# Centred values from TensorE, weight halves ahead of the gates, and a first tile list from four groups

## The reference

```python
q = layernorm(x); k = v = ctx
ig = concat(q, k, v) @ igate_kernel + igate_bias        # one value per token and head
fg = concat(q, k, v) @ fgate_kernel + fgate_bias
log_D = cumsum(log_sigmoid(fg)) - transpose(cumsum(...)) + transpose(ig)   # lower triangle
D = exp(log_D - max(log_D));  C = (q @ k.T / 8) * D
h = (C / (max(|sum C|, exp(-max)) + 1e-6)) @ v
h_norm = (h - mean(h)) * rsqrt(var(h) + 1e-5) * outnorm_scale   # over the 64 features of a head
x = x + h_norm
y = layernorm(x);  top 2 of softmax(y @ router_w.T), weights scaled to sum 1
x = x + sum over the 2 experts of  weight * (gelu(y @ w1[e]) @ w2[e])      # 256 to 1024 to 256
```

## Time and profile before

| what | value |
|---|---|
| time, median of 3 runs | 681.55 us (680.57 to 682.21) |
| profiled execution, its own time | 682.88 us |
| its span, first to last instruction | 681.1 us |
| mean granted TensorE clock | 0.92 of full |
| PE busy | 573.2 us (84%) |
| DVE busy | 400.2 us (59%) |
| ACT busy | 303.1 us (45%) |
| POOL busy | 253.9 us (37%) |
| DMA moved | 118.20 MB |

### The profile page before, as it was taken

How to read it: one execution, slowest core, us unless ns; L and a number is a source line. 1 busy time by engine, 2 the same in 40 slices (tenths; PEclk the granted TensorE clock), 3 DMA queues, 4 the chain that set the end, 5 groups by cost and what they waited for, 6 DMA issues and landing times.

```text
span 681.1 us, 17983 instructions
## 1 busy us (share of the span) xinstructions
PE 573.2 (84%) x5872; PEld 462.7 (68%) x5880; DVE 400.2 (59%) x1146; ACT 303.1 (45%) x585; POOL 253.9 (37%) x194
## 2 busy tenths in 40 slices
PE   1786787777888189979999699989999999999992
PEld 1464566565766178868877578867888888887881
DVE  1469788787887536566567345545555555554550
ACT  2465734626353034544454344434444444444441
POOL 1132238567584405544525422212232233322321
PEclk9796988878787579989999989989999999999997
DMA  9888996694252913636474826598432933295322
GB/s 305 295 322 287 388 323 217 242 322 188 89 209 76 374 56 74 193 71 186 83 194 82 253 43 175 122 328 261 84 53 49 290 50 52 50 319 141 52 25 23
DMA packets 55531, 118.20 MB, mean 174 GB/s; under 512 B 6000, under 2 KB 38000, under 8 KB 54448
## 3 DMA queue, kind: packets, MB, share of 16 engines
q1 hardware_dynamic: 39344, 96.75, 41.0%
q0 software_dynamic: 13392, 18.10, 15.0%
q10 hardware_dynamic: 2736, 2.64, 1.1%
HBM read 188.49 MB, written 40.13 MB: 336 GB/s over the span
## 4 chain that ended last, share of the span: by engine, by line
PE 62%; DVE 11%; issue 7%; ACT 6%; DMA 6%; POOL 3%; SPq 2%; ACTq 1%; DVEq 0%; POOLq 0%
PE bank L706 16%; PE bank L686 9%; PE bank L688 9%; PE bank L687 9%; PE bank L708 8%; PE bank L535 4%; DMA wring<-wsplit 3%; PE bank L609 3%; PE bank L667 2%; ACT xn L795 2%; DVE oh L1132 1%; DVE ct L1029 1%; POOL rows L1462 1%; POOL hrs L1454 1%; DMA rw_all<-in_router_t 1%
## 5 line engine op out<-in xcount | busy, mean ns | idle before, releaser
L1491 POOL DMA_INDIRECT out<-yo,dst x71 | 113.8, 1603 | 286.1 <-DMA out<-yo,dst 156.4
L686 PE MATMUL bank<-wcv,wring 128*128 128x128 f16 x1136 | 202.2, 222 | 16.0 <-DVE wcv L1267 10.1
L1283 DVE TENSOR_TENSOR wcv<-wcv 128x512 f16<-128x512 f32 x142 | 98.3, 692 | 181.8 <-ACT wcv L890 118.8
L687 PE MATMUL bank<-wcv,wring 128*128 128x128 f16 x1136 | 202.3, 222 | 0.0
L688 PE MATMUL bank<-wcv,wring 128*128 128x128 f16 x1136 | 202.3, 222 | 0.0
L706 PE MATMUL bank<-wring,wcv 128*128 128x512 f16 x568 | 193.6, 381 | 0.0
L888 ACT ACTIVATE wcv<-bank 128x512 f32<-128x512 f32 x142 | 84.8, 597 | 213.6 <-PE bank L688 204.2
L708 PE MATMUL bank<-wring,wcv 128*128 128x256 f16 x568 | 155.3, 273 | 0.0
L686 PEld LDWEIGHTS bank<-wcv,wring 128*128 128x128 f16 x1136 | 112.7, 99 | 33.4 <-issue 18.7
L687 PEld LDWEIGHTS bank<-wcv,wring 128*128 128x128 f16 x1136 | 112.7, 99 | 1.5
L688 PEld LDWEIGHTS bank<-wcv,wring 128*128 128x128 f16 x1136 | 112.8, 99 | 0.0
(11 more groups left out here) (148 smaller groups left out, 752.8 us busy)
## 6 DMA issues: line engine op xcount, KB each, us to landing
wring<-wsplit SPq DMA_DIRECT2D x284, 512.0 KB
wring<-in_w SPq DMA_DIRECT2D x16, 1024.0 KB, 12.6
xrow<-rows SPq DMA_DIRECT2D x71, 130.0 KB
wsplit<-wring SPq DMA_DIRECT2D x4, 2048.0 KB, 7.7
wsplit<-wcv SPq DMA_DIRECT2D x4, 2048.0 KB, 7.6
xa<-in_x SPq DMA_DIRECT2D x8, 512.0 KB, 9.4
kT<-in_ctx_t SPq DMA_DIRECT2D x8, 512.0 KB, 8.7
ctn<-in_ctx SPq DMA_DIRECT2D x8, 512.0 KB, 8.6
```

The source lines that it names most:

```text
L686: pe.matmul(o, hi, xT[k][:, c, :], start=(c == 0), stop=False)
L687: pe.matmul(o, hi, xT[k][:, CK + c, :], start=False, stop=False)
L1283: dve.tensor_tensor(gl[o % 2][a][:, :, :], gf[a].rearrange("p (m n) -> p m n", m=4), gh[o % 2][a][:, :, :], ALU.subtract).then_inc(s_glo, 1)
L1491: pool.indirect_dma_start(out=out[:, :], out_offset=bass.IndirectOffsetOnAxis(ap=dst[o][:, 0:1], axis=0), in_=yo[o], in_offset=None, compu ...
```

## The change

- `centre(g)` is now TensorE's: 16 products per group, `kT` (transposed ctx) times a constant 128x128 matrix (identity minus 1/64 within a head's features), give the centred values; ScalarE's `centred` copies them to `vt`. The load `ctn`, GpSimd's subtraction and the four mean columns go away (`GC` is 8 instead of 12), and with them VectorE's wait for `s_vc`.
- In steps T >= 0 the first expert's `weights_high` stands ahead of `log_sigmoid(n)` in ScalarE's program, no longer at the step's end.
- `STAGES` is `{5: (0, 25), 9: (25, 71)}`: the first list comes after T=5, from four groups, with 25 tiles. With it load 7 of `kT` and the store of group 4 go from SyncE to ScalarE.
- The eight pad stores stand one by one between pairs of quarters 16 to 32 of T=9 instead of together behind quarter 24.
- GpSimd scatters one block instead of two ahead of `head_rstd` in steps without tiles; VectorE does `router(l, 0)` ahead of `head_norm`.

```diff
-GC = 3 * NH
+GC = 2 * NH
-STAGES = {6: (0, 33), 9: (33, TILES)}
+STAGES = {5: (0, 25), 9: (25, TILES)}
+C_CEN = C_TRI + P
...
-            def load_c(g):
-                after(sp, s_vc, g - 1)
-                sp.dma_start(ctn[g % 2][:, :, :], ctx_n[:, G * g:G * (g + 1)]).then_inc(s_c[g % 2], 16)
...
+            def centre(g):
+
+                for h in range(2):
+                    o = turn_bank(t_bank(g - 1, h), (s_vc, 2 * g + h + 1))
+                    for b2 in range(2):
+                        for j in range(CK):
+                            mm = pe.matmul(o[:, (2 * b2 + j) * P:(2 * b2 + j + 1) * P], kT[g % 3][:, 2 * h + b2, j, :],
+                                           cst[:, C_CEN:C_CEN + P], start=True, stop=True)
+                    mm.then_inc(s_cen, 1)
...
                 quarters(T, part, 1, 3)
                 if n is not None:
+                    centre(n)
                     cumsum(n)
...
+            def centred(g, h):
+                act.wait_ge(s_cen, 2 * g + h + 1)
+                after(act, s_pv, 4 * (g - 1))
+                act.activation(vt[g % 2][:, 2 * h:2 * h + 2, :, 0:DH],
+                               t_bank(g - 1, h)[:, :].rearrange("p (b h d) -> p b h d", b=2, h=NH), ACT.Copy
+                               ).then_inc(s_vc, 1)
...
                     router_exp(l)
+                if T >= 0:
+                    for e in SPLIT.get(T, ())[:1]:
+                        weights_high(e)
                 if n is not None:
                     log_sigmoid(n)
...
                 if t is not None:
                     values(t, 0)
+                if n is not None:
+                    centred(n, 0)
+                    centred(n, 1)
...
-                quarters(T, part, 16, 20)
-                if m is not None:
-                    router_turned(m, 0)
-                quarters(T, part, 20, 24)
-                if m is not None:
-                    router_turned(m, 1)
                 if T == max(STAGES):
-                    pads()
-                quarters(T, part, 24, 32)
-                for e in SPLIT.get(T, ()):
+                    for e in range(NE):
+                        quarters(T, part, 16 + 2 * e, 18 + 2 * e)
+                        pad_rows_of((e,))
+                else:
+                    quarters(T, part, 16, 20)
+                    if m is not None:
+                        router_turned(m, 0)
+                    quarters(T, part, 20, 24)
+                    if m is not None:
+                        router_turned(m, 1)
+                    quarters(T, part, 24, 32)
+                for e in SPLIT.get(T, ())[0 if T < 0 else 1:]:
                     weights_high(e)
...
-                after(dve, s_vc, g)
...
+                if_l(router, 0)
                 if_m(head_norm)
-                if_l(router, 0)
...
-            def centre(g):
-
-                p = g % 2
-                pool.wait_ge(s_gb, g + 1)
-                pool.wait_ge(s_c[p], 16 * (g // 2 + 1))
-                after(pool, s_pv, 4 * (g - 1))
-                pool.tensor_tensor(vt[p][:, :, :, 0:DH], ctn[p][:, :, :].rearrange("p b (h d) -> p b h d", h=NH),
-                                   gsb[:, :, 2 * NH:GC].unsqueeze(3).to_broadcast([P, G, NH, DH]),
-                                   ALU.subtract).then_inc(s_vc, 1)
...
+    cf[:, C_CEN:C_CEN + P] = np.eye(P) - (part[:, None] // DH == part[None] // DH) / DH
```

More of the change, by code:

```diff
@@ L63 @@
 C_TRI = C_IDENT + P
-C_W8 = C_TRI + P
+C_CEN = C_TRI + P
+C_W8 = C_CEN + P
 C_EBASE = C_W8 + NE
@@ L93, in apart, with build @@
     eng.sem_inc(sem, 1)
-def build(nc, x, ctx_n, ctx_t, gate_w_in, gate_b_in, gamma, rw_t, w1, w2, cf, cb, pad_rows, out):
+def build(nc, x, ctx_t, gate_w_in, gate_b_in, gamma, rw_t, w1, w2, cf, cb, pad_rows, out):
     with ExitStack() as stack:
@@ L129, in build @@
         kT = [sb(f"kT{p}", [P, G, CK, P]) for p in range(3)]
-        ctn = [sb(f"ctn{p}", [P, G, D]) for p in range(2)]
         vt_all = [sb(f"vt{p}", [P, R * VW + WIDE - VW]) for p in range(2)]
@@ L259, in build @@
         s_k = [sem(f"keys_loaded{p}") for p in range(3)]
-        s_c = [sem(f"ctx_loaded{p}") for p in range(2)]
+        s_cen = sem("values_summed")
         s_wst = [sem(f"weights_loaded{p}") for p in range(2)]
@@ L425, in _ @@
             sp.dma_start(gate_b[:, :, :], gate_b_in).then_inc(s_cst, 16)
-            load_c(0)
             load_x(1)
@@ L431, in _ @@
             load_k(1)
-            load_c(1)
             load_w(0)
@@ L480, in step @@
                         load_k(k)
-                        load_c(k)
                     if k + 1 < NG and T < min(STAGES) - 1:
@@ L591, in values @@
                 if b == 0:
-                    pe.wait_ge(s_vc, g + 1)
+                    pe.wait_ge(s_vc, 2 * g + 2)
                     if g < min(BEATS):
@@ L868, in load_kc @@
                 act.dma_start(kT[g % 3][:, :, :, :], ctx_t[:, G * g:G * (g + 1)]).then_inc(s_k[g % 3], 16)
-                act.wait_ge(s_vc, g - 1)
-                act.dma_start(ctn[g % 2][:, :, :], ctx_n[:, G * g:G * (g + 1)]).then_inc(s_c[g % 2], 16)
             def store_x1(g):
@@ L875, in store_x1, with pad_rows_of @@
                               xa[:, G * g:G * (g + 1), :]).then_inc(s_x1o[g], 16)
-            def pads():
+            def pad_rows_of(experts):
                 act.wait_ge(s_pr, 1)
                 act.wait_ge(s_prep, 16)
-                for e in range(NE):
+                for e in experts:
                     r = act.value_load(padr[0:1, e:e + 1], min_val=e * REGION, max_val=e * REGION + NT)
@@ L1499, in step @@
             def step(T, k, n, t, m, l):
-                if n is not None:
-                    centre(n)
                 if m is not None:
@@ L1509, in step @@
                     scatter(l, 0)
-                    scatter(l, 1)
+                    if T in BEATS:
+                        scatter(l, 1)
                 quarters(T, part, 9, 13)
@@ L1518, in step @@
                 if l is not None and T not in BEATS:
-                    scatter(l, 2)
-                    scatter(l, 3)
+                    for b in range(1, G):
+                        scatter(l, b)
                 quarters(T, part, 19, 32)
@@ L1580, in laid_out @@
     gw[:, :, 0:2 * NH] = gates.reshape(3 * CK, P, 2 * NH)
-    for c in range(CK):
-        for q in range(P // DH):
-            gw[CK + c, q * DH:(q + 1) * DH, 2 * NH + c * (P // DH) + q] = 1.0 / DH
     gb = np.zeros((P, G, GC), np.float32)
@@ L1589, in laid_out @@
         "x": x.transpose(1, 0, 2),
-        "ctx": ctx.transpose(1, 0, 2),
         "ctx_t": ctx.reshape(NB, S, CK, P).transpose(3, 0, 2, 1),
```

## The result

| | before | after |
|---|---|---|
| median of 4 runs | 681.06 us (679.49 to 682.21) | 662.77 us (661.65 to 664.39) |
| span of the profiled execution | 681.1 us | 660.2 us |
| first hidden product of tile 0 | 242.27 us | 223.12 us |

The account below looks back on a forecast made before the run. It took a head of engines handing over small results and a tail bound by TensorE. Tile 0's start -5.5, pads -8.9, new stall +9.2, switch -4.4: -9.6 us from 681.55 gives 672.0, range 663 to 681.

Parts of the forecast that it names:

- The stall of expert 3: Step T=1: the moved high halves wait for expert 3's weights, `lf` comes 7.0 us later, +6.0 us net.
- The stall before tile 25: At the list switch, tile 25's rows wait for the last pad store: new stall of 9.2 us.
- The loss at tile 32: At the old list switch, intervals before tiles 32 and 36 lost 4.4 us; this goes, -4.4 us.
- rival (c): Head: `centre` runs at half clock, costing 6.7 us, 3.0 more per group, 24 us in all: 696 us; chance 0.10.
- its own signs: Wrong if steps 2 to 4 differ from 28.4 us by over 1.5; first hidden product at 236.8, no DMA wait.
- `logd` gets back only what it waited for: 0.98 us: Head, step's end: high halves moved ahead give back 0.98 us; with centring's 1.9, net +0.9 us per step.
- Removed are GpSimd's 1.90 us per group, which nobody waited for: Head: taking centring off GpSimd frees 1.90 us per group, credited with no gain.
- Cover 1.8, on the path 1.9 us per step: Head: `centre` takes 3.7 us on TensorE, 1.8 covered before the cumulative sum, 1.9 added per step.
- the 1.1 of the start: Kernel start: one 0.5 MB load fewer ahead of the constants for ScalarE's first norm, -1.1 us.
- The swap of `router(l, 0)` and `head_norm` is free: VectorE's order in the steps: putting `router(l, 0)` first costs nothing, the logits being long there.
- Reason: rows and weights are no longer late: Entry of tile 0: first hidden product 10.0 us behind VectorE's `head_norm` of T=7, was 19.9; gain 11.3 us.
- rival (a): Head steps shorten more, by gates at full clock or TensorE's filled gaps: 666 us, with luck 662; chance 0.18.

Follow-up runs that it names:

- E2: Not a run: the time mark at the end of a group's gate products on TensorE in step T=2.
- E5: Not a run: the time mark at the end of a group's gate products on TensorE in step T=5; 173.7 us before, 163.8 after.
- the third set: Four kernels edited from the changed kernel: GpSimd busy again 669.99 us, centring products doubled 667.17, old tile list 665.15, several edits combined 646.64; kernel before 682.2.
- the first two: Sets of four runs: swap alone, no swap, high halves, scatters (kernel before 712.6 us); changed kernel again, expert 3, `cummax`, rows first (kernel before 713.2).
- second measurement: The changed kernel itself, unaltered, measured again beside three kernels made from it: 692.16 us, ratio 0.9705 to the kernel before.

## Why the prediction was right in sign and half the size

**Right.** The stall of expert 3: forecast `lf` late, the sum at 74, +6.0; the sum came at 70.86, everything having started 3 us earlier, and undoing it alone gave 7.3 in the trace and 8.0 in the median. The pads hidden, -8.9, seen in tiles 21 and 22. The stall before tile 25, 9.2 forecast and 9.3 measured. (The prediction's other figure, 8.4, is an estimate from the Trainium skill, DMA: Bandwidth & Descriptors, Anatomy of one DMA — SWDGE (gpsimd) path; that section gives its fit for DMAs that GpSimd issues, and the last pad and the row load are issued by ScalarE and SyncE.) The loss at tile 32 gone. Centring at full clock but for T=1 (2.37 us for its 16 instructions), so rival (c) never came near its four groups.

By its own signs the prediction was wrong in the head: steps 2 to 4 were to take 28.4 us within 1.5 and took 22.7, 25.9 and 26.5, and the first hidden product was to start at 236.8 with no DMA wait before it and started at 223.12, behind a wait of 6.03.

**The step that failed: "`logd` gets back only what it waited for: 0.98 us, since TensorE's own queue ends there", so "Net per step 1.9 - 1.0 = +0.9 us".** I followed the waits of TensorE to price a step that VectorE sets. In VectorE's timeline stood a wait of 2.61 us for the high halves, which I did not read. The same step has "Removed are GpSimd's 1.90 us per group, which nobody waited for": nobody waited by a semaphore, but VectorE's L1132 took 1.87 instead of 0.16 us under it. The runs put in their place: high halves ahead, some 6 us over four steps; scatters behind `head_rstd`, which I called nothing, 4.4 us; GpSimd free, 5 to 7 us in all by making it busy again (1.7 in the one step of the ledger). From E2 to E5 the change gave -9.5 us where I had next to nothing.

**A term mis-sized: "`centre` is 16 products" and "Cover 1.8, on the path 1.9 us per step".** It is 8 products, 1.95 us (2.37 in T=1), with no wait behind it from T=2 on. A count of a loop's ranges would have told: 2 x 2 x CK is 8. Even at 16 products it cost 3 to 4 us in all. A small term was off as well: 0.5 MB at 400 GB/s is 1.3 us, not the 1.1 of the start.

**"The swap of `router(l, 0)` and `head_norm` is free, the logits being long there."** The logits are not there yet in the tile steps: tiles 7 and 8 took 20.5 instead of 18.3 us, +2.2. In the head it is free, though it takes the wait before the gates away.

**"Reason: rows and weights are no longer late."** They are: SyncE's twelve issues stand ahead of tile 0's rows, and TensorE waited 6.03 us. Against E5 the entry gained 9.3 instead of 11.3, but the list's own share was 5.8, so that the sum came near the forecast partly by luck. As the head ended 9.9 us earlier instead of 5.8 later, this bound came into force sooner.

My rival (a) named the right side and the wrong cause. It priced the gates' clock; the clock did return in T=2 to T=5, but with the swap alone it returned in T=2, T=3 and T=5 and VectorE's steps stayed as long as they were.

## What to carry to other kernels

For a step in which several engines hand work around, write the ledger of the engine that is hardly ever idle over one whole period: every idle time with its releaser, and every instruction whose duration has two values. A wait on another engine, however plain, may be only its shadow: moving the gates and the cumulative maximum changed nothing, while taking VectorE's 2.3 us wait away shortened the step. When an engine's work is removed, ask not only who waits for its result but who shares its ports.

An issue queue is part of the path: eight weight loads ahead of one row load cost 3.5 to 4.4 us.

## What the runs showed of the hardware

- A GpSimd subtraction of 128x1024 float32 (1.90 us) held VectorE instructions with two inputs for nearly its length: 1.86 to 1.87 instead of 0.16 us on 128x32, 1.81 to 1.83 instead of 0.17 on 128x16, in ten cases, five in the kernel before and five in the one with GpSimd busy again. Started 0.8 us behind it, one of 128x16 took 1.16 us, in both kernels.
- It seems to go the other way too: GpSimd's power on 128x16 took 4.91 us where VectorE's low halves ran beside it and 2.94 where VectorE was idle (T=3 with the scatters ahead). This was not tested by itself.
- The kernel before took 681 to 682 us in the result and the third set and 713 in the first two; the three sets ran on three different chips. Some 28 of the 29 us that the changed kernel lost there lie in tiles 2, 3, 10, 11, 18 and 19 (tile 2 took 11.06 instead of 6.40 us), and the kernel before with the swap is slow in the same tiles, with TensorE idle between products for nothing that the profile shows. The cause stays open. TensorE's timeline of the changed kernel in its second measurement:
```profile
252.67 0.22 PE L691 MATMUL bank<-wcv,wring 128*128 128x128 f16 x1 [0.45 <-issue]
253.39 0.22 PE L691 MATMUL bank<-wcv,wring 128*128 128x128 f16 x1 [0.38 <-issue]
```
